# Attention and expert layer: a batch's queries on TensorE moved behind the second half's scores, VectorE's low part of the queries moved behind x1's statistics

## The reference

```python
def _L0_xattn_ref(x, data, Wq, bq, Wkv, bkv, Wp, bp):
    q = (x @ Wq + bq).reshape(bs, n_ctx, HEADS, d)
    kv = (data @ Wkv + bkv).reshape(bs, n_data, HEADS, 2 * d)
    k, v = (kv[..., :d], kv[..., d:])
    scores = jnp.einsum('bqhd,bkhd->bhqk', q, k) * scale
    attn = jax.nn.softmax(scores, axis=-1)
    out = jnp.einsum('bhqk,bkhd->bqhd', attn, v).reshape(bs, n_ctx, WIDTH)
    return out @ Wp + bp
...
x = x + _L0_xattn_ref(_layernorm(x, axis=-1), ctx_1024, ...)
x = x + _L0_ffn_ref(_layernorm(x, axis=-1), ...)
```

## Time and profile before

| | us |
|---|---|
| median of 3 runs | 931.85 (931.54 to 938.29) |
| the profiled execution: its time, its span | 938.24, 936.4 |
| attention rounds 0 to 31, then overlapped with the first expert tile | from 19.8 |

### The profile page before, as it was taken

One profiled execution on the slowest core, in us unless ns is written; L12 is line 12 of the kernel. 1 busy time (PEld: TensorE's weight loads), 2 busy tenths in 40 slices (PEclk: granted clock), 3 DMA queues, 4 the chain that ended last, 5 costly groups with the idle time before them and its releaser, 6 DMA issues.

```text
span 936.4 us, 19131 instructions
## 1 busy us (share of the span) xinstructions
PE 887.6 (95%) x6174; PEld 795.6 (85%) x6174; DVE 745.0 (80%) x1757; ACT 646.3 (69%) x1297; POOL 408.9 (44%) x649
## 2 busy tenths in 40 slices
PE   4999999999998998999999999999999999999995
PEld 3888878887877876788999989899898998998994
DVE  2688888888878888787979788887877877778783
ACT  3676766767666774775977777867776776777773
POOL 3456576777776575330432240605114234052052
PEclk8899999999999999999999999999999999999998
DMA  6332333342255337643756455827817838466442
GB/s 144 66 67 49 74 85 69 86 99 61 63 128 177 114 118 268 182 112 121 217 121 185 135 155 168 240 94 186 278 45 215 282 68 259 177 178 177 147 79 27
DMA packets 132368, 129.17 MB, mean 138 GB/s; under 512 B 59936, under 2 KB 117152, under 8 KB 132128
## 3 DMA queue, kind: packets, MB, share of 16 engines
q1 hardware_dynamic: 119392, 110.36, 38.7%
q0 software_dynamic: 12864, 17.44, 10.3%
HBM read 102.01 MB, written 25.36 MB: 136 GB/s over the span
## 4 chain that ended last, share of the span: by engine, by line
PE 78%; DVE 11%; issue 3%; ACT 3%; another core or an unknown queue 1%; POOL 1%; SPq 1%; DMA 0%; POOLq 0%; DVEq 0%; ACTq 0%
PE bank L1985 35%; PE bank L2029 18%; PE bank L1820 5%; PE bank L1737 4%; PE bank L1977 3%; PE bank L1755 3%; PE bank L1774 2%; DVE maxes L1238 2%; PE bank L1784 2%; PE bank L2017 1%; PE bank L1954 1%; DVE probs L1244 1%; DVE q_l L1279 1%; PE bank L1792 1%
## 5 line engine op out<-in xcount | busy, mean ns | idle before, releaser
L852 POOL DMA_INDIRECT out_rows<-yo,token x68 | 114.4, 1682 | 384.9 <-ACT yo L1095 319.8
L1985 PE MATMUL bank<-xh,wh 128*128 128x512 f32 (+1 forms) x672 | 234.7, 349 | 5.4 <-DVE gate_in L1610 4.8
L1985 PE MATMUL bank<-xl,wh 128*128 128x512 f32 (+1 forms) x672 | 228.9, 341 | 0.0
L1985 PE MATMUL bank<-xh,wl 128*128 128x512 f32 (+1 forms) x672 | 228.5, 340 | 0.0
L1586 DVE TENSOR_TENSOR wl<-raw,wh 128x1024 fp32r<-128x1024 f32 x126 | 152.4, 1220 | 13.0 <-ACT wh L1026 12.1
L1985 PEld LDWEIGHTS bank<-xh,wh 128*128 128x128 f32 x672 | 127.9, 190 | 20.1 <-DVE gate_in L1610 7.5
L2029 PE MATMUL bank<-wh,hh 128*128 128x256 f32 x496 | 141.9, 286 | 1.7 <-issue 1.3
L1985 PEld LDWEIGHTS bank<-xh,wl 128*128 128x128 f32 x672 | 127.8, 190 | 14.9
L2029 PE MATMUL bank<-wh,hl 128*128 128x256 f32 x496 | 140.4, 283 | 0.0
L2029 PE MATMUL bank<-wl,hh 128*128 128x256 f32 x496 | 140.4, 283 | 0.0
L1985 PEld LDWEIGHTS bank<-xl,wh 128*128 128x128 f32 x672 | 128.2, 191 | 10.8
(11 more groups left out here) (195 smaller groups left out, 1861.6 us busy)
## 6 DMA issues: line engine op xcount, KB each, us to landing
raw<-in_W SPq DMA_DIRECT2D x42, 1024.0 KB
raw<-in_Wo SPq DMA_DIRECT2D x25, 1024.0 KB
whole<-in_W SPq DMA_DIRECT2D x8, 1024.0 KB, 7.6
xs<-in_x SPq DMA_DIRECT2D x32, 128.0 KB, 2.7
out_rows<-x SPq DMA_DIRECT2D x32, 128.0 KB, 1.8
shared<-z_rows SPq DMA_DIRECT2D x7, 520.0 KB
bo_row<-in_bo SPq DMA_DIRECT2D x25, 128.0 KB
k_blocks<-k_parts SPq DMA_DIRECT2D x128, 19.2 KB
```

The lines of the kernel that those rows point to most:

```text
L852: e.indirect_dma_start(out=out, out_offset=bass.IndirectOffsetOnAxis(ap=token[j % 4][:, s:s + 1], axis=0), in_=yo[j % 2][:, s, :], in_offs ...
L1985: mm = e.matmul(ps[:, h * cols:(h + 1) * cols], ws[split_before(j) % 2][:, w, c, m * P:(m + 1) * P], xx[j % 2][:, c, 0:cols], start=(h == ...
```

## The change

TensorE: from round 1 on the queries of the next batch are made behind `scores(i,1)` and ahead of the last transposes of the probabilities, in odd rounds. VectorE: in odd rounds the statistics and variance of `x` (tile `i+5`) go ahead of `make_x1`, and `low_queries` goes behind `x1_variance`. Batch 0, which is made ahead of the first scores, stays as it was. ScalarE, GpSimd, the DMA queue and the turns of the banks are as before.

```diff
@@ round_ops of VectorE
-                if batch and not even:
-                    low_queries(nb)
+                if nb == 0 and not even:
+                    low_queries(0)
+                if not even and 0 <= i + 5 < NT:
+                    x_sums(i + 5)
+                    x_variance(i + 5)
                 if 0 <= i - 2 < NT:
                     make_x1(i - 2)
...
                 if 0 <= i - 2 < NT:
                     x1_sums(i - 2)
-                if 0 <= i + 5 < NT:
+                if even and 0 <= i + 5 < NT:
                     x_sums(i + 5)
                 if 0 <= i - 2 < NT:
                     x1_variance(i - 2)
-                if 0 <= i + 5 < NT:
+                if even and 0 <= i + 5 < NT:
                     x_variance(i + 5)
+                if 0 < nb < BATCH and not even:
+                    low_queries(nb)
                 if 0 <= i - 1 < NT:
                     normalized(i - 1)
@@ round_first of TensorE
-                if batch and not even:
+                if i < 0 and batch and not even:
                     queries(nb)
@@ round_second of TensorE
                 if 0 <= i < NT:
                     scores(i, 1)
+                if i % 2 and 0 < i // 2 + 1 < BATCH:
+                    queries(i // 2 + 1)
                 if 0 <= i - 1 < NT:
                     transpose_probs(i - 1, 2)
```

## The result

The median is 937.73 us after (21 runs, 935.54 to 942.47) and 932.72 before (21 runs, 930.76 to 945.07): a ratio of 1.0051 with a 95% interval of 1.0035 to 1.0067. The change costs 5.0 us by the medians and 4.8 by the ratio. That is within the 1% taken as no change, and is well resolved by this number of runs. The profiled execution of after took 938.69 us, its span is 936.9.

A forecast was written before the change was run, and what follows sets the result against it. TensorE was taken as the bound, busy 95% of the span, with 9.5 us of waits for VectorE. Terms +15.5 + 2.8 - 9.5 = +8.8 us on the median 931.85 gave 940.6 us, range 929 to 949.

The forecast's parts named there:

- Scores at 2.37, queries at 2.99: TensorE, odd rounds: scores(i,1) and then queries start this many us after scores(i,0); a gain of nothing by itself.
- Projection behind L927: TensorE, odd rounds: projection waits for ScalarE's queries copy, starting at 5.85 instead of 5.33; +0.5 us per such round.
- q_l behind x1: VectorE, odd rounds: low queries queue behind x1 and delay the next scores; +1.55 us mean over ten rounds, +15.5.
- The delay ends with the DMAs: VectorE, odd rounds with indirect DMAs: x1 stays at 8.49 us, next scores at 10.56, +2.0, taken as +1.55 mean.
- bound below: Odd rounds, projection's signal undelayed: x1 at 7.0, q_l done at 8.75 to 9.3, next scores at 9.1, +0.5 us.
- What comes back in the even round, -9.5: TensorE, even rounds: waits for VectorE go nearly entirely, since x1 and its statistics are already done; -9.5 us.
- Of the pair, the odd round's VectorE is late and the even round's TensorE pays: Rounds 23 and 24: late x1 in the odd round leads to TensorE's 0.96 us gap in the even round.
- Rounds 1 to 9, +2.8: Early odd rounds without indirect DMAs: 4 x 0.65 = 2.6 us in rounds 3 to 9, 0.2 in round 1.
- Nothing waits for them: Odd rounds: no instruction needs the second half's maxima earlier, so moving queries behind scores(i,1) gains nothing by itself.
- No delay on the path: Rival, odd rounds: no late signal, all cost the bound below; -1.7 us in sum, 930.2; chance 0.27.
- The delay follows the projection: Rival, odd rounds: signals 2.2 us late wherever they stand beside the DMAs; +17 us, 949; chance 0.25.
- That nothing is paid: Rival: projection's wait for L927 hidden and VectorE's waits gone; gain at most 9.5 us less a little, 924; chance 0.05.

The follow-up runs named there:

- Kernel 4: After, with the queries from batch 1 on in a score bank instead of the bank shared with the projection: 932.13 us, ratio 0.9998 to before.
- kernel 2: Before with only TensorE's part of the change, VectorE's order as before: 936.61 us, ratio 1.0038.
- Experiment 1: The kernel before, unedited, profiled once more: that execution took 932.19 us.
- kernel 8: After with VectorE's `route` moved from the odd round's end to behind the even round's first-half softmax: 953.68 us, ratio 1.0161 to before.
- 5: Before with VectorE's `route` moved from the odd round's end to behind the even round's first-half softmax: 937.34 us, ratio 1.0004.
- 6: Kernel 4 with `route` moved behind the even round's first-half softmax: 948.50 us, ratio 1.0134 to before.
- 7: Kernel 6 with round 1's queries back at their old place ahead of the second scores: 946.78 us, ratio 1.0113 to before.
- 13: Kernel 10 with the indirect DMAs of the first 8 pairs one round later: 940.24 us, ratio 1.0022 to before.
- Kernel 9: Kernel 8 with GpSimd's four indirect DMAs of a pair issued one round later: 944.20 us, ratio 1.0125 to before.
- 10: Before with `route` behind the value bias in even rounds below 32, old place beyond: 934.68 us, ratio 1.0005.

## Why the prediction came out as it did

The forecast was +8.8, the result +5.0. Two of its terms are wrong, by 9 and by 6 us, and these errors largely cancelled. That the forecast came so near is luck.

- *Scores at 2.37, queries at 2.99*: right to 0.01, except in round 27.
- *Projection behind L927*: right, and it is most of the loss. Forecast 5.85, measured 5.91. The scores follow at 9.15 where 9.08 was worked out; over rounds 5 to 25 it is +0.6 for the +0.5 forecast. Kernel 4 shows it as the cause, kernel 2 that TensorE's part alone brings it.
- *q_l behind x1*: the step that failed is "The delay ends with the DMAs, as the rows of GpSimd suggest, at the same place as before", +1.55 in each of ten rounds. The "bound below" held from round 5 on: x1 at 7.05 to 7.23 (7.0 there), q_l done ahead of the scores, by 0.4 where it is short and by 0.05 where it is long. Round 27 is the exception, all of it 1.3 later behind its wait for L1244. In rounds 11 to 29 the odd rounds have +6.4 in place of the +15.5. Experiment 1 shows why the row misled: the waits of the earlier trace rows are not in a second profile of the same kernel.
- *What comes back in the even round, -9.5*: measured -3.0 in waits for L1244 (8.1 to 5.1), and -3.6 by round times. Of the 9.5, the 1.4 for attn belong to the one execution; experiment 1 has no such wait. The sentence that failed for the rest is "Of the pair, the odd round's VectorE is late and the even round's TensorE pays". VectorE's chain can't start ahead of the values' end, however early x1 is: in sum over the twelve even rounds from 8 to 30, `recip` comes 2.7 us sooner after than in experiment 1, and the chain behind it was 1.5 shorter. And `recip` to maxima was read as 2.19 in round 24, near the lowest; the mean over these rounds is 2.5 in the first profile, 2.8 in experiment 1 and 2.7 after. In round 24 it is 2.72 and 2.60 in the latter two, nearly all of the difference in two short operations, `pick` and `gates` (0.74 and 0.60 in place of 0.22 from the first's start to the next operation). With the 0.1 ahead of `recip` and the 1.3 behind the maxima VectorE needs about 4.0 to 4.1 there, where TensorE has 3.4.
- *Rounds 1 to 9, +2.8*: with +0.05 in round 3 and +0.64 to +0.69 in 5, 7 and 9 it is +2.0 without round 1. Round 3 pays nothing, since there queries and projection don't share a bank. Most of what round 1 showed goes with the clock.
- *Round 27*: it isn't in the sum. "Nothing waits for them" held for the queries' readers, but the queries had covered TensorE while VectorE was late. It is +0.85 of the +8.4.
- *The rivals.* "No delay on the path" had the right course and, by too large a gain in the even rounds, the wrong sign (-1.7). Of the two reasons that it gives, a burst of queries and the profiler, neither is shown. "The delay follows the projection" never occurred in after, but kernel 8 shows such a delay at the queries. That nothing is paid is excluded by the 4.7 us of waits.

Round by round against experiment 1 the sum is +8.4 - 3.6 = +4.8.

What stays open: why TensorE's signals are late in some executions and orders beside indirect DMAs (before's first profile, and kernels 5 to 8 and 13) and not in after, where the same four run from 223.58 to 228.51 beside queries and projection. That the delay ends with the DMAs fits only some of it. In rounds 13, 15, 17 and 21 of kernel 8, x1 starts 1.0 us behind the end of the last; but the copies of the queries start 0.5 ahead of that end in round 23 and 0.2 behind it in round 25. Kernel 9 shows that where the DMAs lie matters, not by what means.

## What to carry to other kernels

Ahead of moving a group of instructions on one engine, write down the deal of the shared banks: what counts is the distance between the bank's last user and its next claimant, here 1.26 us cut to 0.64 where 0.96 is needed. A wait that starts a theory should be seen in a second profile of the same kernel before it is multiplied by ten rounds. And to say which late step causes a wait, follow the chain back to the instruction that had no slack (here `recip`, which begins when the values end), not to the one with the longest wait. And a list of waits by line mixes rounds: 9.4 to 7.7 hid a fall from 8.1 to 5.1 in the even rounds behind a new wait in an odd one.

## What the runs showed of the hardware

**The granted clock goes with the spread.** In 23 runs of before on one chip, 930.34 to 937.84 us, the mean granted clock goes from 0.994 to 0.985, a correlation of -0.85. Rounds 0 and 1, behind the idle start, lie at a clock that differs by execution: after's profile, then experiment 1's, a window in round 1:

```profile
30.00:34.00 4.00, 4.00 (x22) 3.29 (x19) 2.15 (x6) 2.36 (x5) 1.50 (x4) 0.74 0.70 133
```

```profile
30.00:34.00 4.00, 3.99 (x32) 3.26 (x31) 2.37 (x6) 3.97 (x10) 1.80 (x4) 1.00 0.60 113
```

Of the kernels that have the moved queries too, 2, 6, 8 and 9 show 1.00 in this window and 4 shows 0.87. Their round 1 is 0.3 shorter to 0.4 longer than experiment 1's, after's is 1.5 longer. So most of the 2.4 us that rounds 0 and 1 are longer in this profile is no part of the change's price.

**A wait of TensorE can be followed by the lower clock, which costs more than the wait.** Behind waits of 2.50, 1.59 and 2.22 us (kernels 8, 5 and 10) the granted clock was 0.50, and the same 20 products of the values took 4.37, 4.51 and 4.51 us instead of 2.35. In kernels 5 and 10 wait and clock together made up the 5.9 and 5.6 us of two rounds. Behind the wait of 1.29 in round 27 of after the clock stayed up.

**A short operation on VectorE isn't always equally long.** `gates` took 0.66 in experiment 1's round 24 and 0.25 in after's, the cast of `pick` 0.24 and 0.51. In both, GpSimd's six products ran beside; in the first profile of before they did so too, in part, and the two took 0.22 and 0.17. What decides it isn't shown.
